# One change in four parts to a fused tower kernel: when big transfers are issued, how padding rows are written, which PSUM banks the features use, and idle products

## The reference, cut to what matters

```python
h = tok(x)                                   # S4D-style features: V = exp(dA_log*l), K = 2*einsum('chn,hnl->chl', Ct, V).real
h = concat([cls_tok, h], axis=1)             # 16 sequences x (1+256) tokens x 512
h = h + attn(layernorm(h), ...)              # gates = u@W_in; scan h = (1-a)*h + a*b over tokens; y@W_out + x@W_skip + biases
h = h + ffn(layernorm(h), ...)               # shared expert (704 wide) + top 2 of 8 routed experts (352 wide each)

def ffn(x):                                  # x: 4112 tokens x 512
    scores = softmax(x @ gate_w)
    topk_w, topk_idx = top_k(scores, 2)
    routed = sum over the two experts e of topk_w * ((silu(x @ w_gate[e]) * (x @ w_up[e])) @ w_down[e])
    shared = (silu(x @ sw_gate) * (x @ sw_up)) @ sw_down
    return routed + shared
```

## Time and profile before

| what | value |
|---|---|
| median of three runs | 1199.46 us (1191.7 to 1201.67) |
| the profiled execution | 1196.48 us |
| its span, first to last instruction | 1194.8 us |
| PE busy | 1059.5 us, 89% |
| DVE busy | 812.2 us, 68% |
| POOL busy | 383.9 us, 32% |
| ACT busy | 347.2 us, 29% |
| mean granted TensorE clock | 0.944 |
| DMA, mean over the span | 154 GB/s |

### The profile page before, as it was taken

One profiled execution on the slowest core, in us unless ns is written; L12 is line 12 of the kernel. 1 busy time (PEld: TensorE's weight loads), 2 busy tenths in 40 slices (PEclk: granted clock), 3 DMA queues, 4 the chain that ended last, 5 costly groups with the idle time before them and its releaser, 6 DMA issues.

```text
span 1194.8 us, 26490 instructions
## 1 busy us (share of the span) xinstructions
PE 1059.5 (89%) x7869; PEld 696.9 (58%) x7870; DVE 812.2 (68%) x2123; ACT 347.2 (29%) x658; POOL 383.9 (32%) x352
## 2 busy tenths in 40 slices
PE   3046898999999999999999994989999999999995
PEld 3034566666766676667766771655555555555552
DVE  7976988898889888988898563544444444444442
ACT  4413433443344333443344332111111111111110
POOL 1011221222123211332022210145545656655554
PEclk8556998999999999999999997899999999999998
DMA  7322456455545555455535589689998777877885
GB/s 247 112 53 54 105 159 154 124 152 173 149 127 150 170 151 143 139 171 162 165 112 157 170 258 371 188 170 217 224 172 132 130 130 130 134 132 128 133 124 74
DMA packets 311150, 183.57 MB, mean 154 GB/s; under 512 B 261218, under 2 KB 280034, under 8 KB 309044
## 3 DMA queue, kind: packets, MB, share of 16 engines
q1 hardware_dynamic: 292948, 135.83, 46.8%
q0 software_dynamic: 15504, 36.46, 15.2%
q10 hardware_dynamic: 2640, 10.54, 2.3%
HBM read 53.40 MB, written 79.73 MB: 111 GB/s over the span
## 4 chain that ended last, share of the span: by engine, by line
PE 75%; DVE 3%; SPq 3%; DMA 3%; issue 2%; ACT 1%; POOLq 0%; POOL 0%; ACTq 0%; DVEq 0%
PE bank L997 30%; PE bank L1146 10%; PE bank L1156 10%; PE bank L1147 10%; PE bank L1072 8%; PE bank L1011 4%; DMA out<-x2w,rows_in 2%; SPq L779 1%; SPq L781 1%; PE bank L1076 1%; ACT tokens L1202 1%; PE bank L1062 1%; DMA wexp<-w_halves 1%; PE bank L1075 1%; DVE wexp L1351 0%
## 5 line engine op out<-in xcount | busy, mean ns | idle before, releaser
L997 PE MATMUL bank<-wexp 128*128 128x256 f16 (+2 forms) x3252 | 418.6, 291 | 24.8 <-issue 9.5
L997 PEld LDWEIGHTS bank<-wexp 128*128 128x128 f16 x3252 | 316.4, 101 | 110.7 <-issue 33.7
L1146 PE MATMUL bank<-wexp,rows_in 128*128 x852 | 255.5, 313 | 9.6 <-issue 6.9
L1147 PE MATMUL bank<-wexp,rows_in 128*128 x852 | 255.1, 312 | 0.0
L975 POOL DMA_INDIRECT out<-x2w,rows_in x71 | 113.7, 1601 | 116.0 <-DMA out<-x2w,rows_in 82.8
L927 POOL TENSOR_TENSOR inv<-var,power 128x4 f32<-128x4 f32 x17 | 29.2, 1717 | 375.0 <-DVE var L1533 375.0
L1689 DVE SCALAR_TENSOR_TENSOR mixed<-bank,mixed 128x352 f32<-128x352 f32 x71 | 37.2, 525 | 161.0 <-ACT mixed L1308 108.4
L963 POOL TENSOR_TENSOR ex<-base,ld 128x8 f32<-128x8 f32 x71 | 120.7, 1699 | 75.9 <-DVE ld L1668 56.0
L1146 PEld LDWEIGHTS bank<-wexp,rows_in 128*128 128x128 f16 x852 | 83.1, 98 | 66.6 <-issue 25.9
L1308 ACT ACTIVATE mixed<-bank 128x352 f32<-128x352 f32 x71 | 32.9, 464 | 295.3 <-PE bank L1147 295.3
L1156 PE MATMUL bank<-wexp,gates 128*128 (+1 forms) x477 | 111.7, 379 | 2.9 <-DVE x2w L1684 2.9
(11 more groups left out here) (281 smaller groups left out, 1247.3 us busy)
## 6 DMA issues: line engine op xcount, KB each, us to landing
w_halves<-rows_in SPq DMA_DIRECT2D x16, 704.0 KB
wexp<-w_halves ACTq DMA_DIRECT2D x1, 8704.0 KB
wexp<-w_halves SPq DMA_DIRECT2D x8, 1088.0 KB
h_tok<-tokens SPq DMA_DIRECT2D x16, 512.0 KB, 2.7
mixed<-h_tok SPq DMA_DIRECT2D x32, 256.0 KB
out<-h SPq DMA_DIRECT2D x32, 256.0 KB
w_halves<-rows_in SPq DMA_DIRECT2D x16, 384.0 KB
rows_in<-in_L_ffn_w_gate SPq DMA_DIRECT2D x16, 352.0 KB, 5.4
```

Source lines behind the costliest of these rows:

```text
L997: last = MM(dst, stat_of(step, a), mov_of(step, b), start=(s_ == 0 and a + b == 0), stop=(s_ == len(steps) - 1 and a == 1))
L1146: MM(GB[:, 0:H], xT[b][:, a, c, :], wexp[:, u, o:o + H], start=s_, stop=e_)
L1147: last = MM(UB[:, 0:H], xT[b][:, a, c, :], wexp[:, u, o + H:o + 2 * H], start=s_, stop=e_)
```

## The change

1. The 8.7 MB load of the first four experts' weights (ACT, queue q10) is issued at the start of round 15 and no longer at its end.
2. The padding rows: the DRAM table `pads` now holds whole rows. Its data part, zeros, is written by four transfers on SP at the end of round 1 (8 x 128 x 2048 bytes each). `pad_rows` is then one copy from DRAM to DRAM instead of a copy of the tails and a write of zeros. The pads of expert 4 are issued between the two `wexp<-x3w` copies of round 16.
3. `BU` is now `BD`. `features` waits for `c_dev` (both down products of the round read) instead of `c_gm`; the wait for `c_toke` moves from `gate_up_shared(0)` to `gate_up_shared(2)`.
4. PE makes products whose result nobody reads: 36 before the first features, 10 before the first `project`, 28 before the second `input_project` (128x512 f16 each).
5. The units of the upper half of `wexp` are loaded one for every three expert tiles and no longer one for every two; SP's unrolled part grows from 16 to 24 tiles.

```diff
-    pads_d = nc.dram_tensor("pads", [E, 4, P, 16], I32).ap()
+    pads_d = nc.dram_tensor("pads", [E, 4, P, XW], F16).ap()
...
-        BU = [psum[1], psum[2]]
         BH = [psum[1], psum[2], psum[0]]
         BD = [psum[3], psum[0]]
+        BU = BD
...
-            eng.dma_start(xs_d[bass.ds(row, 3 * P), 2 * D:XW].bitcast(I32),
-                          pads_d[e].rearrange("r q w -> (r q) w")[bass.ds(turn, 3 * P)]).then_inc(c_z, 16)
-            eng.dma_start(xs_d[bass.ds(row, 3 * P), 0:2 * D].bitcast(I32).rearrange("(i p) w -> p i w", p=P),
-                          zrow[:, 0:2 * D].bitcast(I32).rearrange("p (o w) -> p o w", o=1).broadcast_to([P, 3, D])).then_inc(c_z, 16)
+            eng.dma_start(xs_d[bass.ds(row, 3 * P), :], pads_d[e].rearrange("r q w -> (r q) w")[bass.ds(turn, 3 * P), :]).then_inc(c_z, 16)
...
+                            if i == 1 and isinstance(k, int) and k == NCH:
+                                pad_rows(sp, 4)
...
-                        for e in range(4, 6):
-                            pad_rows(sp, e)
+                        pad_rows(sp, 5)
...
+                    if isinstance(k, int) and k == 1:
+                        for r in range(4):
+                            sp.dma_start(pads_d[:, r, :, 0:2 * D].bitcast(I32).rearrange("e q w -> q e w"),
+                                         zrow[:, 0:2 * D].bitcast(I32).rearrange("p (o w) -> p o w", o=1).broadcast_to([P, E, D])).then_inc(c_pw, 16)
...
-                    if isinstance(i, int) and i < 2 * E and i % 2:
-                        u = E + i // 2
+                    if isinstance(i, int) and i < 3 * E and i % 3 == 1:
+                        u = E + i // 3
...
-                        pe.wait_ge(c_gm, k * 6)
+                        pe.wait_ge(c_dev, k * 2)
...
+                        if m == 2:
                             at_least(pe, c_toke, clampc(k + 1) * 2)
-                        if m == 2:
                             at_least(pe, c_dev, n * 2)
...
+                    def idle_products(count):
+
+                        for i in range(count):
+                            MM(BD[0][:], ident16[:], wskip[:, 0, 0, :], start=True, stop=True)
+
                     if isinstance(k, int) and k == -1:
+                        idle_products(36)
                         features(k)
+                    if isinstance(k, int) and k == 0:
+                        pe.wait_ge(c_toke, 2)
+                        idle_products(10)
...
+                    if isinstance(k, int) and k == 0:
+                        idle_products(28)
                     if first_win:
                         input_project()
...
                 def body(k, q):
+                    if isinstance(k, int) and k == NCH - 1:
+
+
+                        act.wait_ge(c_tokm, NCH * 2)
+                        act.wait_ge(c_wo, 32 * E)
+                        act.dma_start(wexp[:, 0:E, :], w16_d[0:E].rearrange("u p n -> p u n")).then_inc(d_w, 16)
```

More of the change, by code:

```diff
@@ L828, in body @@
                         sp.wait_ge(c_ri, 1)
-                        sp.wait_ge(c_pw, 64)
+                        sp.wait_ge(c_pw, 128)
                         for e in range(4):
@@ L879, in body @@
                         for r in range(4):
-                            sp.dma_start(pads_d[:, r].rearrange("e q w -> q e w"), pads[:]).then_inc(c_pw, 16)
+                            sp.dma_start(pads_d[:, r, :, 2 * D:XW].bitcast(I32).rearrange("e q w -> q e w"), pads[:]).then_inc(c_pw, 16)
                 iterate(sp, body)
@@ L900, in _ @@
                 sp.wait_ge(d_w, 16)
-                over_tiles(sp, serve, 2)
+                over_tiles(sp, serve, 3)
                 for b in range(2):
@@ L936, in body @@
                         if isinstance(k, int) and k == LAST:
-                            gp.wait_ge(c_z, 32 * E)
+                            gp.wait_ge(c_z, 16 * E)
                         apart(gp, c_sep)
@@ L1254, in body @@
                         act.wait_ge(c_ri, 1)
-                        act.wait_ge(c_pw, 64)
+                        act.wait_ge(c_pw, 128)
                         pad_rows(act, 6)
@@ L1294, in body @@
                         gate_tanh()
-                    if isinstance(k, int) and k == NCH - 1:
-                        act.wait_ge(c_tokm, NCH * 2)
-                        act.wait_ge(c_wo, 32 * E)
-                        act.dma_start(wexp[:, 0:E, :], w16_d[0:E].rearrange("u p n -> p u n")).then_inc(d_w, 16)
                 act.wait_ge(c_cst, 2)
```

## The result

The changed kernel takes 1201.04 us (median of 13 runs, 1198.44 to 1206.25), the kernel before, on the same chip, 1195.80 (13 runs, 1187.94 to 1201.67). The ratio is 1.0048, 95% interval 1.0025 to 1.0071: slower by half a per cent. The forecast was 8.7 us faster, with a range of 1171 to 1204 and chances of 0.47 for a gain of over 1%, 0.46 for anything within 1%. The time lies inside the range; the direction is wrong.

A forecast was written before the change was run, and what follows sets the result against it. PE sets the pace in rounds 3 to 14, a serial PE-DVE chain and then DVE in the first rounds. The terms -7 + 15.3 - 7 - 5 + 13 - 14 - 4 sum to -8.7 us: 1190, range 1171 to 1204.

The forecast's parts named there:

- Idle products: First rounds: products nobody reads warm the clock, so features, gate products and projections run faster; -7 us, full effect 8.7.
- doesn't warm the clock: First rounds: the 36 products end too early; +5 us, 1195; counted within the forecast's chance of 0.55.
- Zeros: Round 1: pad zeros between store and load of features delay DVE, and so PE, in round 2; +15.3 us, 11 to 18.
- Expert tiles: First expert tiles: loads for every three tiles take the DMA share to just under 1; -4 us, between -6 and 0.
- Banks: Rounds: features in the down products' banks end PE's wait for tokens, -7 us, and most clock drops, -5.
- the split into 7 and 5: Of the banks' gain, 7 us from PE's vanished waits for tokens, 5 from clock drops that go with them.
- Early load: Round 15: the big weight load delays the load of features, for which DVE and then PE wait; +13 us, 0 to 17.
- rows of pads: Round 16: pads freed of the big load let the second turned copy land earlier and PE restart near 734.5; -14 us.
- Rival 1: Round 15: the load of features slips through beside the big load, landing near 680; 11 us less, 1179; chance 0.2.
- Rival 2: Round 1: the zeros hide, part or all of 15 us; 1175 alone, 1164 with features slipping through; chance 0.13 together.
- Rival 3: Round 16: pad copies within DRAM are slow, above 4.4 us each; at 5 us the 14 are lost, 1205; chance 0.12.
- the likeliest case: The forecast itself, including the clock staying cold: 1190, own range 1182 to 1199; chance 0.55.

The follow-up runs named there:

- e1: The changed kernel without its 36, 10 and 28 idle products: 1202.36 us, ratio 1.0061.
- e15: The changed kernel with 44, 10 and 44 idle products instead of 36, 10 and 28: 1197.11 us, ratio 0.9992.
- e12: The kernel before with features in the down products' banks and 44, 10 and 44 idle products: 1180.19 us, ratio 0.9845.
- e4: The kernel before with only features in the down products' banks and the wait for tokens moved to the third gate-up group: 1182.22 us, ratio 0.9881.
- e2: The changed kernel with its zeros written one per round, in rounds 1, 2, 3 and 14, behind the weight loads: 1185.27 us, ratio 0.9896.
- e7: The changed kernel with the upper units loaded one per two expert tiles again: 1204.72 us, ratio 1.0064.
- e10: e2 with the early load halved to four units, the other twelve one per three expert tiles: 1174.83 us, ratio 0.9809.
- e14: e6 with old pads, late units one per four tiles, 8 idle products before round 2's features, load split between round 15's start and end: 1167.40 us.
- e11: The changed kernel with the pads of before, two copies per expert and no zeros in the table: 1181.72 us, ratio 0.9870.
- e3: The changed kernel with the 8.9 MB load of the first experts' weights back at the end of round 15: 1197.43 us, ratio 1.0002.
- e8: The changed kernel with the early load cut into two DMAs on the same queue, pieces half the size: 1203.13 us, ratio 1.0034.
- e6: The changed kernel with zeros spread, four units loaded at round 15's end, twelve one per three tiles, 44, 10 and 44 idle products: 1168.78 us, ratio 0.9769.
- e5: The changed kernel with zeros spread and the full load issued by ACT behind the normalisation of round 15's features: 1183.29 us, ratio 0.9873.

## Why the prediction was wrong

Most mechanisms stood; the sum of their sizes did not, and one saving had the wrong owner. The terms lay on both sides of zero, 37 us of gains against 28.3 of losses, and every one in the table came out on the bad side of its estimate. No single one turns the sign: the idle products (4.9 us), the zeros (2.9) and the expert tiles (2.8) do it together.

1. **Idle products: -7 forecast, -2.1 measured** (e1; the table's -4.0 has 2.2 from the banks in it). This is the step that failed most. The forecast booked the features at their warm 3.79 us and the gate products at 2.18 (measured 5.94 and 3.24), and 2 us from a warm `input_project` (none came). It had the 36 end "near 71", and the features begin at 73.25. The 2.3 us between were in its own numbers, and no row of before shows a warm engine after such a pause; it weighed a pause only for the 28. With 44, 10 and 44 products the term is -6.7 (-2.05 and e15's -4.65) and -6.8 by e12 against e4 (638.75, 645.51): the size was right for such a kernel, and the one forecast on had 36, 10 and 28. The rival "doesn't warm the clock" had +5 and no chance of its own; in the main it is what happened, since only the first `project` ran warm (2.75 us instead of 5.28).
2. **Zeros: +15.3, measured +18.2.** Mechanism as told, e2 confirms the place. DVE waited 19.1 us, not 15.3: the load landed 28.4 us after the store's issue (144.14 to 172.57) instead of 26.0, and DVE was ready 5.4 us earlier than before, the store only 4.0.
3. **Expert tiles: -4, measured -1.2.** The idle time of the first tiles fell by 3.7 us, and 1.5 of it came back behind them. The stage varies by some 5 us between profiles of like kernels (e7), so neither the forecast's figure nor the measured one is known to a microsecond.
4. **Banks: -12, measured -11.35 in rounds 3 to 14, -13.0 in all** (e4). Right as a sum, clock drops included; the split into 7 and 5 wasn't measured: the nine rounds between the features of rounds 3 and 12 take 343 us in nearly every kernel with this edit (344.7 in e10 and e14), 353.0 before (228.01 to 581.02).
5. **Early load +13, measured +14.2; rows of pads -14, measured -13.2.** Right in place and size, and with the wrong owner. The forecast booked the -14 to the padding rows; e11 gives them nothing, e3 shows the wait of 18.4 us back as soon as the load is. The right statement is that the early load costs 14.2 and saves 13.2. That this came out near the forecast's sum of the two is luck.

These make 11.4 us. The other 2.5 between -8.7 and +5.2 are the profiled executions' distance from the medians, within the scatter of single runs. The absolute 1190 had another fault: it rested on three runs of before with a median of 1199.46. Thirteen give 1195.80, the profiled execution lies 0.7 us above that and not 3.0 below, and on this level the forecast is 1187.

Rival 1 (the features slip through the big load, 0.2) fell: they landed at its end, at 693.7. The rule of the Trainium skill named beside it ("DMA: Bandwidth & Descriptors", Queues, rings and completion order) has an engine change queues only at packet boundaries of several descriptors; the small queue's 0.6 to 0.8 pieces per big one in e8 and in the changed kernel are a mean and don't show the size of a turn, so the rule is neither borne out nor refuted. Rival 2 (zeros hide, 0.13) fell, though e2 shows that they can be hidden by moving them. Rival 3 (copies within DRAM over 4.4 us each) fell: four are issued in 7.30 us, the second turned copy is issued 17.0 us behind the first pad (729.48, 746.48; the forecast had 17, the rival over 30), and PE's wait is 6.1 us. Each copy took 5.3 to 9.2 us from issue to landing, several at a time. The 358 GB/s in that rival is no limit here: from 677 to 685 us the kernel moved 423, nearly all of it weights read from DRAM. No rival but the fourth touched what happened: the mechanisms nearly as told, each size somewhat worse, which is 11 us here. Whether the common sign of the six errors is chance isn't shown. A sum of six terms with an error of 2 to 3 us each has an error of 6, and the likeliest case's own range of 1182 to 1199 around -8.7 left no loss in it.

## What to carry to other kernels

Put a bulk transfer where nothing short stands behind it or beside it for its whole length, and if there is no such place, cut it by bytes, not by pieces, and send only what is needed first: four units instead of eight at the end of round 15 (e6) made the way from the features of round 14 to the expert tiles 17.0 us shorter than in e2 (eight, at its start) and 11.3 shorter than in e3 (eight, at its end). The expert stage with its four more late loads takes 422.4 to 424.5 us in five profiles, mean 423.6, against 420.5 with eight late ones: some 3 us of it go back. Idle products must last until the work that they warm; count the pause behind them, not the products. When a change has several parts, measure each: one of five made 13 us of gain, one made 18 of loss for nothing, and the two that seemed to belong together (early load, new pads) did not.

## What the runs showed of the hardware

- Short pauses went with a slower restart, by degrees. Between the 36 products and the features PE idled 1.4 to 1.7 us in e3, e8 and e10, with the features at 3.79 us; 2.0, 2.3, 2.7 and 2.9 us go with 4.7, 5.3, 5.9 and 6.4, and 7.09 is the time without products. The pause differs by a microsecond between kernels that are the same up to there, and what follows then begins up to 3.5 us later (106.86 in the changed kernel, 103.41 in e3). Later in the program the same pause went with different times (3.79 and 5.11 us with 1.18 and 1.19).
- Beside a load of 8,704-byte pieces SP's queue got 3.3% of the engines' time with 256-byte pieces (0.06 of 3.4 MB in 8 us). Halving the big pieces took its share to 8.2%, and the store landed 0.8 us sooner, the features no sooner.
- SP's issuing instructions grow long behind or beside big transfers: 12.6 us for the two loads behind the zeros, 12.1 for a store of weights beside the early load (677.47), 18.6 us for the two turned copies beside the load in e5, against 0.4 to 3 us for the same transfers with nothing big near them. This stands in the trace as a long DMA instruction, not as a wait of SP.
